# Layer 1's first sums and moments placed at the end of the experts' stage, and its chunk loop in another order

## What is computed

```python
x = L0_attn_X
xn = _layernorm(x, axis=-1)
s = attention(xn);  g = _silu(experts(xn))
x = x + s * g
xn = _layernorm(x, axis=-1)
s = recurrence(_rmsnorm(xn, norm_w), dt, A, Bmat, C, D)   # decay exp(-sigmoid(dt)*|A|)
g = _silu(fp4_linear(silu(fp4_linear(xn, w_gate)) * fp4_linear(xn, w_up), w_down))
x = x + s * g
```

## Time and profile before

| | us |
|---|---|
| median of 3 runs | 1958.31 |
| the three runs | 1952.79, 1958.31, 1962.83 |
| the profiled execution | 1953.15 |
| its span in the trace | 1951.3 |
| start of layer 1 in it | 1763.87 |
| start of chunk 0's body on DVE | 1799.58 |
| mean granted TensorE clock | 0.971 |

### The profile page before, as it was taken

One profiled execution on the slowest core, in us unless ns is written; L12 is line 12 of the kernel. 1 busy time (PEld: TensorE's weight loads), 2 busy tenths in 40 slices (PEclk: granted clock), 3 DMA queues, 4 the chain that ended last, 5 costly groups with the idle time before them and its releaser, 6 DMA issues. The chain is left out here.

```text
span 1951.3 us, 33300 instructions
## 1 busy us (share of the span) xinstructions
PE 1816.0 (93%) x10467; PEld 1044.8 (54%) x10467; DVE 1516.1 (78%) x2052; ACT 1006.9 (52%) x1506; POOL 1434.1 (73%) x870
## 2 busy tenths in 40 slices
PE   5899999999999999999999999999999799974677
PEld 4455555555555555555555555555554577762446
DVE  7877777777777777777777777777777778878885
ACT  4345445445544544544454444554454678865542
POOL 4388888888888888888888888888888265745553
PEclk9899999999999999999999999999999899987887
DMA  7101010100101010101011010101010676330000
GB/s 243 45 12 55 19 54 22 43 30 36 54 11 54 11 55 11 62 13 52 22 44 54 11 54 11 54 12 59 13 54 22 221 222 213 108 111 24 6 17 22
DMA packets 98438, 108.95 MB, mean 56 GB/s; under 512 B 8161, under 2 KB 88097, under 8 KB 95202
## 3 DMA queue, kind: packets, MB, share of 16 engines
q1 hardware_dynamic: 93410, 98.26, 15.3%
q0 software_dynamic: 4992, 10.27, 1.5%
HBM read 53.12 MB, written 27.38 MB: 41 GB/s over the span
## 5 line engine op out<-in xcount | busy, mean ns | idle before, releaser
L1300 POOL TENSOR_TENSOR psum_k<-psum_k,probs 128x1024 f32<-128x1024 f32 x384 | 925.9, 2411 | 200.2 <-ACT probs L1245 185.1
L1317 DVE TENSOR_REDUCE mxh<-ps_m 128x2 f32<-128x1024 f32 x518 | 633.3, 1223 | 254.1 <-PE ps_m L1077 252.7
L1245 ACT ACTIVATE probs<-ps_s 128x1024 f32<-128x1024 f32 x512 | 497.3, 1023 | 263.9 <-PE ps_s L1094 214.4
L1102 PE MATMUL ps_v<-probs,V 128*64 128x512 f32 x2056 | 489.8, 597 | 0.0
L1341 DVE RECIPROCAL rden<-den 128x128 f32<-128x128 f32 x260 | 245.6, 946 | 25.6 <-ACT den L1214 16.0
L1102 PEld LDWEIGHTS ps_v<-probs,V 128*64 128x64 f32 x2056 | 137.3, 137 | 235.6 <-issue 231.1
L1077 PE MATMUL ps_m<-k_hi,q_hi 64*128 64x512 f32 x1036 | 237.5, 451 | 10.9 <-DVE mxh L1317 7.2
L1092 PE MATMUL ps_s<-q_lo,k_hi 64*128 64x512 f32 x1024 | 203.0, 389 | 0.0
L1094 PE MATMUL ps_s<-shift,ones_r 64*128 64x512 f32 x1024 | 202.8, 388 | 0.0
L1092 PE MATMUL ps_s<-q_hi,k_lo 64*128 64x512 f32 x1024 | 202.3, 389 | 0.0
L1092 PE MATMUL ps_s<-q_hi,k_hi 64*128 64x512 f32 x1024 | 202.2, 390 | 0.0
(11 more groups left out here) (304 smaller groups left out, 2783.0 us busy)
## 6 DMA issues: line engine op xcount, KB each, us to landing
e_ew<-w_split SPq DMA_DIRECT2D x23, 1024.0 KB
V<-V_next SPq DMA_DIRECT2D x33, 512.0 KB, 3.3
xs_hi<-xh SPq DMA_DIRECT2D x16, 512.0 KB, 3.7
xs_lo<-xl SPq DMA_DIRECT2D x16, 512.0 KB, 4.3
rows<-in_blank_d SPq DMA_DIRECT2D x4, 1483.5 KB, 16.7
e_x_raw<-rows SPq DMA_DIRECT2D x23, 258.0 KB
we_raw<-in_experts_d SPq DMA_DIRECT2D x33, 128.0 KB, 2.4
w_split<-we_hi SPq DMA_DIRECT2D x32, 128.0 KB, 1.9
```

The source lines that it names most:

```text
L1102: ins = nc.tensor.matmul(ps_v[rows, :], V[par][:, kt, rows], probs[:, t % RING, x, :], start=kt == 0, stop=kt == KT - 1)
L1245: nc.scalar.activation(probs[:, t % RING, :, :], ps_s[t % 2][:, :, :], ACT.Exp, scale=SCALE).then_inc(p_done, 1)
L1300: nc.gpsimd.tensor_tensor(acc, probs[:, (t - 1) % RING, :, :] if kt == 1 else acc, probs[:, t % RING, :, :], ALU.add).then_inc(add_done, 1)
L1317: nc.vector.tensor_reduce(mxh[:, kh, t, :], max_bank(unit, i)[:, :, :], AX.X, ALU.max).then_inc(m_done, 1)
```

## The change

What it does, engine by engine:

- **Experts' end, DVE**: `moments(0)` now stands between `weighted` of chunk 5 and `gated(4)`, and `moments(1)` between `gated(5)` and `weighted` of chunk 7. The sum is written in place into `x_tok`. **PE**: `attended` 4 to 7 come after the first of the last five `down`. **POOL**: `inverses` is split in `inverse_std` and `inverse_rms`; both of batch 0 run here. **ACT**: `normalise(0)` stands between `gate(6)` and `gate(7)` and writes into two buffers of the experts' rows (`xn_early`).
- **Experts' first tiles**: SP loads `dt` and `A` after the second tile's weights, ACT's first exponential is in tile 1, DVE's five `decays` steps in tile 2, ACT's second exponential in tile 3. The four constants that remain are waited for later. The Exp table load, the second Silu load and the warming SiLU in layer 1 go.
- **Layer 1's start**: DVE begins with `quantise` of chunk 0, ACT with `rms_rows(0)`, POOL with `inverse_std(1)`; its `inverse_rms(1)` comes after the first scaled rows. X of batches 2 and 3 goes to a buffer of its own.
- **Chunk loop**: on DVE `gated(c - 2)` follows the last step of A instead of preceding ACT's sizes; on ACT `gate(c - 2)` follows `sizes` of A in body c instead of ending body c - 1; on POOL `finish(c - 2)` follows the scaling of A. In body 0 ACT copies `xqT` of chunk 2 before the sizes of B and `normalise(2)`; in body 3 `hidden_T` and `input_T` stand ahead of the sizes. `recurrences` is [4], [5, 6], [7] in bodies 5 to 7 instead of [4, 5], [6, 7], none, and in bodies 6 and 7 `down(c - 1)` comes before them.

The diff, cut to its core:

```diff
+def moments(nc, v, g, b):
+    x = g.gate[:, b * T:(b + 1) * T]
+    if b < 2:
+        for k in range(T // CH):
...
+            ins = nc.vector.tensor_tensor(part, part, g.y_row[b * (T // CH) + k][:, :, :].rearrange("p t d -> p (t d)"), ALU.add)
...
             rows = tail(3, NS)
             token_rows(*rows.pop(0))
-            for i, q in tail(LAG, NB):
+            for n, (i, q) in enumerate(tail(LAG, NB)):
                 down(i, q)
+                if n == 0:
+                    for v in range(EARLY_A - 1, NCH):
+                        attended(v)
                 if q % FT == 0:
                     token_rows(*rows.pop(0))
-            for v in range(EARLY_A - 1, NCH):
-                attended(v)
...
             gate(NCH - 2)
+            act.wait_ge(xt_ready, ROUTED)
+            act.wait_ge(at_done, ROUTED)
+            normalise(nc, act, g, 0)
             gate(NCH - 1)
...
+            pool.wait_ge(g.var_done, 1)
+            inverse_std(nc, pool, g, 0)
+            inverse_rms(nc, pool, g, 0)
...
-            for n, (i, s) in enumerate(tail(3, NS)):
-                weighted(i, s)
-                gated(NCH - 4 + n)
+            last = tail(3, NS)
+            weighted(*last[0])
+            v.wait_ge(a_done, 2)
+            moments(nc, v, g, 0)
+            gated(NCH - 4)
+            weighted(*last[1])
+            gated(NCH - 3)
+            v.wait_ge(a_done, 4)
+            moments(nc, v, g, 1)
+            weighted(*last[2])
+            gated(NCH - 2)
             gated(NCH - 1)
...
-        return ([], [0], [1], [2], [3], [4, 5], [6, 7], [])[c]
+        return ([], [0], [1], [2], [3], [4], [5, 6], [7])[c]
+
+    def recurrences_last(c):
+        return c >= LAST - 1
...
                 sizes(q_h[0], steps_before(c) + 4)
+                if c >= 2:
+                    gate(c - 2)
+                    if recurrences_last(c - 1):
+                        for k in recurrences(c - 1):
+                            recurrence(k)
...
                 step_A(2, 2)
                 step_A(3, 3)
-                if not no_result(c):
-                    gated(c - 2)
                 v.wait_ge(size_done, sizes + 1)
                 step_A(5, 0)
                 step_A(6, 5)
+                if not no_result(c):
+                    gated(c - 2)
...
+                    if recurrences_last(c):
+                        down(c - 1)
                     if recurrences(c):
                         pe.wait_ge(hT_done, c)
                     for k in recurrences(c):
                         recurrence(k)
-                    down(c - 1)
+                    if not recurrences_last(c):
+                        down(c - 1)
...
             chunks(body)
+            pe.wait_ge(y_done, NCH)
             last_hidden_T(0)
```

256 lines of the change are left out of this document (137 added, 119 removed).

## The result

The changed kernel takes **1942.67 us** (median of 6 runs, 1938.09 to 1945.23) against 1956.2 us for the kernel before (6 runs on the same chip, 1952.24 to 1963.53). The ratio is **0.9924, with a 95% interval of 0.9902 to 0.9947**: 14.9 us less, well outside half a per cent at the middle and just outside it at the nearer end. The forecast was 1941.

The account below looks back on a forecast made before the run. DVE was taken as fullest nearly everywhere in the last 212 us, PE in bodies 6 and 7. Terms -6.7, -1.6, -2.0, -4.5 and +0.5 sum to -14.3 us; from a middle of 1955.7, 1941 us, range 1931 to 1953.

Parts of the forecast that it names:

- part 3: Bodies 0 and 1: copying chunk 2's `xqT` earlier on ACT shortens DVE's waits for the gates; -1.6 us, 0 to -2.6.
- part 4: Bodies 2 to 5: `pr` after A's last step removes waits and slow `val` steps; -2.0 us, +4 to -4.
- part 5: Bodies 6, 7 and the end: `down` ahead of the recurrences shortens waits before `pr`; -4.5 us, -1.8 to -8.
- Parts 1 and 2: Experts' end and layer 1's start: moments moved into DVE's idle time, first projection sooner; together -6.7 us, -5.5 to -8.
- with some 0.3 for hand-offs: Experts' end: an estimated 0.3 us for hand-offs, within layer 1 starting 4.3 us later.
- the hole isn't filled: Rival, experts' end: PE's transposes come late, so the moments cost 7.7 us, not 4.3; 1944.5; shares 0.56 with the forecast.
- the credit for body 5's earlier `down`: Body 5: `down` comes one recurrence sooner, 2.5 us at the low clock.
- Part 6: Experts' first tiles: two tiny transfers and DVE's five steps added there; +0.5 us, 0 to +1.
- My own signs of being wrong: Body 0 not at least 5 us sooner, rounding in the loop costing more, or lower clock in bodies 1 to 5.
- Collisions: Rival, bodies 2 to 7: `pr` collides with POOL's scaling, 6 x 0.95 = 5.7 us; 1946; chance 0.16.
- The gain stops at the start: Rival: DVE is late from chunk 0 on, so parts 3 to 5 bring about -1; about 1950; chance 0.15.
- Slower, by the low clock in a dense body: Rival: a new idle stretch of PE leaves the clock low through two dense bodies, 12 us each; 1965; chance 0.06.

Follow-up runs that it names:

- e11: Kernel before with only ACT's order in body 3 changed, copies ahead of the sizes of the rest; ratio 0.9987 to the kernel before.
- e13: The changed kernel run again unaltered, as a measure for runs on the same chip; ratio 0.9931 to the kernel before.
- e2: Changed kernel with PE's transposes of chunks 4 to 7 put back behind the experts' last `down`; median 1925.84 us.
- e8: Changed kernel with POOL's rms of batch 0 made first thing in layer 1, not at the experts' end; median 8.7 us below that of e7.
- e5: Changed kernel with `pr` first again, ACT's gate at the body's end and POOL's `finish` at its front; ratio 0.9914 to the kernel before.
- e9: Changed kernel with batch 0's rms made on POOL after chunk 0's scaling, and `down` back behind the recurrences; ratio 0.9881 to the kernel before.
- e10: Changed kernel with only ACT's order in body 3 taken back, sizes of the rest ahead of the copies; median 1944.6 us.
- e12: Changed kernel with batch 0's rms made on POOL after chunk 0's scaling, its order of `down` and recurrences kept; ratio 0.9923 to the kernel before.
- e1: Changed kernel with the eight bodies in the order of the kernel before, the new start kept; ratio 0.9961 to the kernel before.
- e7: Changed kernel with ACT's sizes (and body 0's normalising) ahead of the input copy again in bodies 0 and 3; ratio 0.9953, median 1943.35 us.

## Why the prediction was right, point by point

**The total was right, and for the loop that was luck: some 3 us of part 3 were left out, part 4 brought half of its term, and the 4.1 us saved in bodies 6 and 7 were not part 5's.** The sum was -14.3; the profiled pair differs by 15.0 in the tail, and the ratio makes 0.0076 x 1956.2 = 14.9. The start was -6.7 and came to -6.0; parts 3 to 5 were -8.1, and from body 0 on the tail is 9.0 us shorter.

- *Parts 1 and 2, -6.7: measured -6.0* in the profiled pair; against e11, whose start is that of the kernel before, e13 on the same chip gains 5.0. The hole was filled (the experts' end on DVE moved by 3.7 us, from 13.1 to 16.8 after `weighted(5)`; forecast 4.0). From layer 1's first step to body 0 it took 35.6 and takes 24.2: 11.4 gained, forecast 11.0. The first projection comes 8.3 after the stage's start, forecast 8.4. What failed is the step "with some 0.3 for hand-offs": the change of blocks cost 1.7 more than before, because POOL, which had stood idle since the experts' last squares, now works until 6 us before the end. I had looked at POOL's steps as lying beside DVE's moments, and hadn't asked what POOL does after them. The rival *the hole isn't filled* didn't come true; e2 shows that the moved transposes are worth 1.1 us of wait, though none of the time.
- *Part 3, -1.6: right for body 0, and blind for body 3.* Bodies 1 and 2 together took 34.0 and take 32.4 to 32.8 in eight traces (33.3 in the profiled one and in e8): -1.3 to -1.6, or -0.7. But the same edit takes 3 out of `(0, 1, 3)`, and I worked out only 0. In the kernel before PE stood 6.84 us in body 3:

```profile
1867.78 1.54 PE L2116 MATMUL ps_b<-wT_gu,xqT 128*128 128x352 f32 x2 [6.84 <-ACT xqT L1816]
```

  and after the change:

```profile
1856.28 0.86 PE L2175 MATMUL ps_b<-wT_gu,xqT 128*128 128x352 f32 x2 [1.70 <-ACT xqT L1906]
```

  So chunk 5's projection goes into the hole, and the `down` behind it, which began 3.3 us inside body 4 (1874.09), begins 2.9 us before it (1860.98). Body 4, which PE had bounded, is DVE's: 17.7 to 14.6 by this half alone (e11). The row was in the same timeline that I had read for body 0.
- *Part 4, -2.0: measured -0.9* (e5 against e13, bodies 2 to 5). The wait before the sizes is there in all bodies, as forecast (0.86, and 1.09 in body 2 of the profiled trace). What failed is the credit for body 2: the gate's wait and the slow `val` step are gone, but POOL's scaling of A and `finish` now run beside B's two multiplies (1.58 and 1.75 where 0.83 and 0.68 stood before), and body 2 is no shorter. The 0.86 that I charged to bodies 3 and 5 did not appear as time either: there `pr` had taken 1.64 in the kernel before (see the collisions below), and it takes 0.68 now. And the wait of 2.65 in body 4 that I booked here goes by part 3: it isn't there in e11 either, where `pr` stands first.
- *Part 5, -4.5: no gain by itself on top of parts 3 and 4.* Bodies 6 and 7 did become 4.1 shorter (46.0 to 41.9). But with part 5 back they take 39.0 (42.25 in e9, beside the late rms), with part 4 back 41.1, with part 3 back 42.3. The wait of 5.89 in body 6 is gone in all three runs that leave one part out, and 2.34 or less is left of the 4.67 in body 7; only e9, with the clock at 0.71 in body 6, waits 2.82 and 2.57. So any two of the parts are enough, or nearly. No run has part 3 alone; e11, with half of it, still waits 4.44 and 4.66. Adding up "what this wait was" and "what that part removes" books the same slack twice. The step that failed is the credit for body 5's earlier `down`; nor is a recurrence 2.5 us at the low clock, as I read from rows 11: PE takes 2.1 for it at full clock and 4.0 at half.
- *Part 6, +0.5: not measured.* `weighted(5)` stands at 1750.32 after 1750.45, but on one chip it stands at 1758.74 in e11, without part 6, and at 1754.98, 1754.91 and 1753.67 in e13, e10 and e12, with it. The term cannot be told from this scatter.
- *My own signs of being wrong.* Two of the three appeared without the total being wrong: the rounding in body 2 costs more (the two multiplies above), and the clock in body 1 fell, from 0.89 to 0.85 (0.79 in e13), while it rose in bodies 3 and 5 from 0.84 and 0.88 to 1.00. The upper end of the range counted part 4 as +1, where its own term went to +4.

**The rivals.** *Collisions*: refuted, `pr` took 0.68 or 0.69 in all six bodies. Such a collision is real all the same, and it stood in the trace of before, in bodies 3 and 5, where I had looked only for waits. In body 3 POOL had begun first:

```profile
1853.18 1.80 POOL L1718 TENSOR_TENSOR q_x_val<-q_x_val,q_x_m 128x512 f32<-128x512 f32 x1
...
1853.89 1.64 DVE L2064 TENSOR_TENSOR pr<-sT,g 128x512 f32<-128x512 f32 x1
```

Nor is a DVE step longer whenever both engines run, as I wrote: the reduction at 1843.00, beside POOL's 1.52 from 1842.84, took its usual 0.87. The rule of the Trainium skill that I weighed (SBUF — State Buffer, "Who interferes with whom") is not contradicted by the changed kernel: where the two met, `pr` had begun first and POOL's multiply was the longer one, as in body 6. Its rows on POOL, the first of A's scaling in bodies 6 and 7:

```profile
1897.79 1.84 POOL L1837 TENSOR_TENSOR q_h_val<-q_h_val,q_h_m 128x704 f32<-128x704 f32 x1 [3.02 <-DVE q_h_val L1669]
...
1914.25 1.52 POOL L1837 TENSOR_TENSOR q_h_val<-q_h_val,q_h_m 128x704 f32<-128x704 f32 x1 [5.99 <-PE ps_a L2206]
```

The same section adds that it is the order of issue that decides who blocks, and the trace agrees: `pr` had begun at 1897.57, 0.22 us ahead of POOL, and kept its 0.68. I had taken it for the loser without asking which of the two starts first. *The gain stops at the start*: e1 says no by its times, though its one trace came out so. *Slower, by the low clock in a dense body*: this exists, at 4.6 us in e1's body 4 and 5.1 in e7's body 2, and not at the 12 I priced it, since the clock comes back within the body. And it came where I had not looked: in the dense bodies 2 and 4 the long falls are in traces that keep an order of the kernel *before* (e1, e7, e11). Behind the new idle stretch of 7.72 us in body 1 the clock was low for some 3 us (eight transposes took 1.97 instead of 1.09) and then full again. It was low once more, for some 4 us, in the projections at the edge of body 2, where body 2 took 18.9 us instead of 17.2; that was behind 2.22 us of idle time only.

**What stays open.** No run has parts 1 to 3 without 4 and 5. Since taking back either one costs nothing that the times show, such a kernel may be as fast as the changed one; that is a guess. And which half of part 3 makes up the 7.4 us by which e7 is slower is shown for body 4 alone.
